# A preactivation convolution on one core: three image rows summed by an overlapping load and VectorE, and output stores issued by GpSimd

## The reference

```python
def _conv(x, w): return lax.conv_general_dilated(x, w, (1, 1), [(1, 1), (1, 1)],
                        dimension_numbers=('NCHW', 'OIHW', 'NCHW'))
# x: (16, 256, 56, 56) f32, conv_w: (256, 256, 3, 3)
v = group_norm(x, G=32, eps=1e-5)
xn = (v - mean(v)) * rsqrt(var(v) + 1e-4) * bn_gamma + bn_beta   # mean, var over n, h, w
t = jnp.where(xn >= 0.0, 1.0, 0.0)
t = jnp.where(xn <= 0.0, -1.0, t)
c_sum = jnp.sum(jnp.clip(xn, -1.0, 1.0) * t, axis=1, keepdims=True)
c_cnt = jnp.sum(jnp.abs(t), axis=1, keepdims=True)
y = _conv(t, conv_w) + conv_b
b_sum = _conv(c_sum, ones(1, 1, 3, 3)) + beta_conv_b
b_cnt = _conv(c_cnt, ones(1, 1, 3, 3)) + beta_conv_b
out = x + y * (b_sum / b_cnt)
```

## Time and profile before

| | before |
|---|---|
| time, median of 3 runs | 962.09 us (962.08 to 962.1) |
| profiled execution, its own time | 963.27 us |
| profiled execution, first to last instruction (span) | 961.4 us |
| busy PE / DVE / ACT / POOL | 798.8 / 784.3 / 587.8 / 106.0 us |
| from 600 to 940 us: PE busy | 340.0 of 340 us |
| HBM read, written | 180.39 MB, 51.78 MB |

### The profile page before, as it was taken

One profiled execution on the slowest core, in us unless ns is written; L12 is line 12 of the kernel. 1 busy time (PEld: TensorE's weight loads), 2 busy tenths in 40 slices (PEclk: granted clock), 3 DMA queues, 4 the chain that ended last, 5 costly groups with the idle time before them and its releaser, 6 DMA issues. The chain is left out here.

```text
span 961.4 us, 13260 instructions
## 1 busy us (share of the span) xinstructions
PE 798.8 (83%) x4750; PEld 469.3 (49%) x4750; DVE 784.3 (82%) x1224; ACT 587.8 (61%) x472; POOL 106.0 (11%) x97
## 2 busy tenths in 40 slices
PE   2100004997999999999999999999999999999996
PEld 2100002554555555555555555555555555555553
DVE  4999997886878787878787878787878787879844
ACT  2043005894777777768686868686868686868410
POOL 0099200000000000000000000000000000000010
PEclk9655556998999999999999999999999999999999
DMA  9999962258979797979798879888888888876697
GB/s 360 431 392 395 412 258 70 71 206 204 298 184 282 189 278 195 273 198 268 207 267 208 261 195 266 219 256 215 254 210 239 233 261 208 264 172 175 158 225 211
DMA packets 41522, 232.41 MB, mean 242 GB/s; under 512 B 8608, under 2 KB 8736, under 8 KB 37408
## 3 DMA queue, kind: packets, MB, share of 16 engines
q1 hardware_dynamic: 31712, 181.43, 51.4%
q0 software_dynamic: 9072, 50.58, 29.0%
q10 hardware_dynamic: 720, 0.18, 0.1%
HBM read 180.39 MB, written 51.78 MB: 241 GB/s over the span
## 5 line engine op out<-in xcount | busy, mean ns | idle before, releaser
L540 PE MATMUL acc<-V,U 128*128 128x385 f16 (+1 forms) x4608 | 776.9, 331 | 17.5 <-DVE V L756 12.1
L540 PEld LDWEIGHTS acc<-V,U 128*128 128x128 f16 x4608 | 449.3, 98 | 333.9 <-issue 16.7
L420 ACT ACTIVATE sn<-acc,inv_s 128x784 f32<-128x784 f32 x128 | 116.7, 913 | 217.0 <-PE acc L540 213.8
L324 POOL DMA_DIRECT2D y<-x x63 | 54.5, 865 | 791.4 <-DVE y L825 774.2
L825 DVE SCALAR_TENSOR_TENSOR y<-y,vec,bmap 128x1568 f32<-128x1568 f32 (+1 forms) x65 | 117.4, 1809 | 8.0 <-DMA bmap<-map_rows 7.8
L399 ACT ACTIVATE r<-xb,ab 128x1568 f32<-128x1568 f32 x64 | 106.5, 1691 | 6.7 <-DVE ssum L763 3.1
L378 ACT ACTIVATE u<-xb,ab 128x1624 f16<-128x1624 f32 x64 | 110.5, 1730 | 0.1
L388 ACT ACTIVATE T<-u 128x1680 f16<-128x1680 f16 x60 | 95.6, 1594 | 5.1 <-DVE D L749 5.0
L390 ACT ACTIVATE T<-T 128x1568 f16<-128x1568 f16 x60 | 90.6, 1511 | 1.9
L749 DVE TENSOR_TENSOR D<-T 128x1568 f16<-128x1568 f16 x64 | 62.4, 975 | 28.5 <-ACT T L390 28.5
L505 PE MATMUL csum<-mv,cst 128*128 128x32 f32 x2 | 0.6, 398 | 94.9 <-DVE mv L625 94.9
(11 more groups left out here) (92 smaller groups left out, 363.6 us busy)
## 6 DMA issues: line engine op xcount, KB each, us to landing
xb<-x SPq DMA_DIRECT2D x64, 812.0 KB, 6.2
y<-x POOLq DMA_DIRECT2D x63, 784.0 KB, 8.2
out<-y SPq DMA_DIRECT2D x63, 784.0 KB, 6.2
y<-x SPq DMA_DIRECT2D x16, 1568.0 KB, 8.3
bmap<-map_rows SPq DMA_DIRECT2D x32, 784.0 KB, 6.0
xb<-x SPq DMA_DIRECT2D x14, 1568.0 KB, 8.6
V<-w_t SPq DMA_DIRECT2D x2, 1152.0 KB, 14.4
out<-y SPq DMA_DIRECT2D x2, 392.0 KB, 2.3
```

The lines of the kernel that those rows point to most:

```text
L420: nc.scalar.activation(sn[:, b, half], acc[:, b, :, 0:N], ACT.Copy, scale=inv_s[:, b:b + 1])\
L540: last = nc.tensor.matmul(by_row(acc[:, g % 2, bank, 0:N])[:, :, lo:hi], U[:, ci, digits, k, dx, co * P:(co + 1) * P], by_row(V[:, a, ci, ...
```

## The change

- `crow` becomes 56 x 3 x 58: one load brings to each partition the row above, its own row and the row below, from overlapping windows of `sum_rows` (`row_windows`). For that `sum_rows` has a row of zeros above and below each image, written once at the start from ScalarE's queue.
- VectorE adds the three rows (`vsum`, a reduction of 3 x 58 values in each partition), then three columns, then bias and count, all in one function `beta_map` where `columns` stood. TensorE's `boxed`, its band matrix and the semaphore `box_done` are gone.
- GpSimd issues the stores of the first 63 pieces: after the accumulating transfer of piece s it waits for that of s - 1 to land and stores piece s - 1. SP's stores of these pieces are gone. SP still stores the two parts of the last one.
- SP's loop over pairs of images is written out.

```diff
-    x_pairs = x_rows[1:NI - 1].rearrange("(i k) c p f -> i k c p f", k=2)
+    row_windows = bass.AP(sum_rows.tensor, 0, [[(H + 2) * W, NI], [W, H], [1, 3 * W]])
...
-        crow = sb("crow", [H, W + 2])
+        crow = sb("crow", [H, 3, W + 2])
+        vsum = sb("vsum", [H, W + 2])
...
-                sp.dma_start(sum_rows[m].rearrange("(h k f) -> k h f", h=2, f=SQ), cs49[:, :, :])\
+                sp.dma_start(sum_rows[m, W:W + H * W].rearrange("(h k f) -> k h f", h=2, f=SQ), cs49[:, :, :])\
                   .then_inc(cs_stored, 16)
                 sp.wait_ge(cs_stored, 16 * m + 16)
-                at_least(sp, hsum_ready, m)
-                sp.dma_start(crow[:, 1:W + 1], sum_rows[m].rearrange("(r w) -> r w", w=W)).then_inc(crow_in, 16)
-
-            def store(n, g):
-                sp.wait_ge(x_added[g], 16 * n + 16)
-                sp.dma_start(out_v[n, g % 2, g // 2], y[:, g]).then_inc(y_out[g], 16)
+                at_least(sp, vsum_ready, m)
+                sp.dma_start(crow[:, :, 1:W + 1], row_windows[m].rearrange("r (k w) -> r k w", w=W))\
+                  .then_inc(crow_in, 16)
...
-                store(n - 1, 0)
                 crow_load(n)
-                store(n - 1, 1)
...
-            with sp.Fori(0, (NI - 4) // 2) as i:
-                image(2 * i + 1, x_pairs[i + 1, 0])
-                image(2 * i + 2, x_pairs[i + 1, 1])
-            image(NI - 3, x_rows[NI - 1])
+            for n in range(1, NI - 2):
+                image(n, x_rows[n + 2])
...
+            def store(s):
+
+                n, g = divmod(s, G4)
+                pool.wait_ge(x_added[g], 16 * n + 16)
+                pool.dma_start(out_v[n, g % 2, g // 2], y[:, g]).then_inc(y_out[g], 16)
+
             for s in range(G4 * NI - 1):
                 n, g = divmod(s, G4)
                 pool.wait_ge(scaled, s + 1)
                 pool.dma_start(y[:, g], x_v[n, g % 2, g // 2], accum_op=ALU.add).then_inc(x_added[g], 16)
+                if s:
+                    store(s - 1)
+            store(G4 * NI - 2)
...
+            act.wait_ge(pads, 4)
+            act.dma_start(sum_rows.rearrange("n (r w) -> n r w", w=W)[:, 0:H + 2:H + 1], crow[0:NI, 0:2, 0:W])\
+               .then_inc(zeros_in, 16)
...
-            def boxed(n):
-
-                pe.wait_ge(hsum_ready, n + 1)
-                at_least(pe, bm_ready, n)
-                nc.tensor.matmul(box[:, 0:W], cst[0:H, C_TRI:C_TRI + P], hsum[:, 1, :],
-                                 start=True, stop=True).then_inc(box_done, 1)
...
-            def columns(n):
+            def beta_map(n):
 
                 dve.wait_ge(crow_in, 16 * n + 16)
-                nc.vector.tensor_tensor(hsum[:, 0, :], crow[:, 0:W], crow[:, 1:W + 1], ALU.add)\
-                  .then_inc(hpart, 1)
+                nc.vector.tensor_reduce(vsum[:, :], crow[:, :, :].rearrange("r k w -> r w k"), AX.X, ALU.add)\
+                  .then_inc(vsum_ready, 1)
+                dve.wait_ge(vsum_ready, n + 1)
+                nc.vector.tensor_tensor(hsum[:, 0, :], vsum[:, 0:W], vsum[:, 1:W + 1], ALU.add).then_inc(hpart, 1)
                 dve.wait_ge(hpart, n + 1)
-                at_least(dve, box_done, n)
-                nc.vector.tensor_tensor(hsum[:, 1, :], hsum[:, 0, :], crow[:, 2:W + 2], ALU.add)\
+                nc.vector.tensor_tensor(hsum[:, 1, :], hsum[:, 0, :], vsum[:, 2:W + 2], ALU.add)\
                   .then_inc(hsum_ready, 1)
-
-            def beta_map(n):
-
-                dve.wait_ge(box_done, n + 1)
+                dve.wait_ge(hsum_ready, n + 1)
                 at_least(dve, bm_stored, 16 * n)
-                nc.vector.scalar_tensor_tensor(
-                    out=bm[:, :], in0=box[0:H, 0:W], scalar=bb[0:H, :], in1=rcount[:, :],
-                    op0=ALU.add, op1=ALU.mult)\
-                  .then_inc(bm_ready, 1)
+                nc.vector.scalar_tensor_tensor(out=bm[:, :], in0=hsum[:, 1, :], scalar=bb[0:H, :], in1=rcount[:, :],
+                                               op0=ALU.add, op1=ALU.mult).then_inc(bm_ready, 1)
```

More of the change, by code:

```diff
@@ L28 @@
 FIRST, SECOND, THIRD = (1, 3), (2, 4), (0, 5)
-C_GROUP, C_TRI, C_COUNT = 0, P, P + P
+C_GROUP, C_COUNT = 0, P
 C_FOLD = C_COUNT + W
@@ L111, in conv_preact @@
         y_out = [sem(f"y_out{g}") for g in range(G4)]
+        last_out = [sem(f"last_out{k}") for k in range(2)]
         x_added = [sem(f"x_added{g}") for g in range(G4)]
@@ L126, in conv_preact @@
                              "cs_stored", "crow_in"))
-        hpart, hsum_ready, box_done, bm_ready, bm_stored = (
-            sem(s) for s in ("hpart", "hsum_ready", "box_done", "bm_ready", "bm_stored"))
+        zeros_in = sem("zeros_in")
+        vsum_ready, hpart, hsum_ready, bm_ready, bm_stored = (
+            sem(s) for s in ("vsum_ready", "hpart", "hsum_ready", "bm_ready", "bm_stored"))
         bmap_in = [sem(f"bmap_in{h}") for h in range(2)]
@@ L231, in map_load @@
                 sp.dma_start(bmap[:, h, :],
-                             map_rows[bass.ds(n, 1), h * HPX:(h + 1) * HPX].to_broadcast([P, HPX]))\
+                             map_rows[n:n + 1, h * HPX:(h + 1) * HPX].to_broadcast([P, HPX]))\
                   .then_inc(bmap_in[h], 16)
@@ L251, in image @@
                     load(n, ahead, 1)
-                store(n - 1, 2)
                 map_load(n, 1)
@@ L255, in image @@
                     load(n, ahead, 2)
-                store(n - 1, 3)
                 if ahead is not None:
@@ L261, in _ @@
                 first_load(g)
+            sp.wait_ge(zeros_in, 16)
             crow_load(0)
@@ L267, in _ @@
                 load(0, x_rows[2], g)
-            with sp.Fori(0, (NI - 4) // 2) as i:
-                image(2 * i + 1, x_pairs[i + 1, 0])
-                image(2 * i + 2, x_pairs[i + 1, 1])
-            image(NI - 3, x_rows[NI - 1])
+            for n in range(1, NI - 2):
+                image(n, x_rows[n + 2])
             image(NI - 2)
             image(NI - 1)
-            for g in range(3):
-                store(NI - 1, g)
             for k, (lo, hi) in enumerate(LAST_PARTS):
                 sp.wait_ge(last_added, k + 1)
-                sp.dma_start(out_v[NI - 1, 1, 1][:, 4 * lo:4 * hi], y[:, 3, 4 * lo:4 * hi]).then_inc(y_out[3], 16)
+                sp.dma_start(out_v[NI - 1, 1, 1][:, 4 * lo:4 * hi], y[:, 3, 4 * lo:4 * hi]).then_inc(last_out[k], 16)
             for g in range(G4):
-                sp.wait_ge(y_out[g], 16 * (NI + (g == 3)))
+                sp.wait_ge(y_out[g], 16 * (NI - (g == 3)))
+            for k in range(2):
+                sp.wait_ge(last_out[k], 16)
         @block.gpsimd
@@ L589, in _ @@
             third(0, 0, 1)
-            boxed(0)
             second(0, 0, 2)
@@ L615, in _ @@
             nc.vector.memset(u[:, :, 0:UR:UR - 1], 0.5).then_inc(pads, 1)
-            nc.vector.memset(crow[:, :], 0.0).then_inc(pads, 1)
+            nc.vector.memset(crow[:, :, :], 0.0).then_inc(pads, 1)
             nc.vector.memset(eps[:, 0:1], GN_EPS)
@@ L658, in _ @@
             nc.vector.tensor_scalar(mxb[:, :], mxb[:, :], 2.0 ** -14, None, ALU.mult).then_inc(wrow, 1)
-            nc.vector.memset(crow[:, 0:1], 0.0).then_inc(wscale, 1)
+            nc.vector.memset(hsum[:, 0, 0:1], 0.0).then_inc(wscale, 1)
             for k in range(8, 12):
@@ L848, in _ @@
             transform(1, 1, 0)
-            columns(0)
+            beta_map(0)
             ends(0, 1)
-            beta_map(0)
             pair_sum(1, 0)
@@ L882, in image @@
                     if g == 0:
-                        columns(n)
+                        beta_map(n)
                     if prep and g == 1:
@@ L915 @@
     rows = np.arange(H)
-    consts[:H, C_TRI:C_TRI + H] = abs(rows[:, None] - rows[None, :]) <= 1
     near = 3.0 - (rows == 0) - (rows == H - 1)
@@ L931 @@
     args = {name: nc.dram_tensor(name, v.shape, F32, kind="ExternalInput").ap() for name, v in arrays.items()}
-    sum_rows = nc.dram_tensor("sum_rows", (NI, H * W), F32, kind="Internal").ap()
+    sum_rows = nc.dram_tensor("sum_rows", (NI, (H + 2) * W), F32, kind="Internal").ap()
     map_rows = nc.dram_tensor("map_rows", (NI, H * W), F32, kind="Internal").ap()
```

4 lines of the change are left out of this document (removed).

## The result

| | before | after |
|---|---|---|
| median of the runs | 962.09 us (961.41 to 962.1, 4 runs) | 949.62 us (949.5 to 950.02, 4 runs) |
| ratio to before | | 0.987, 95% interval 0.9858 to 0.9881 |
| profiled execution, its own time | 963.27 us | 950.02 us |
| span | 961.4 us | 948.0 us |

The change takes 12.5 us, where 13.1 were forecast, and the time is 949.62 us, where 949.0 were.

What follows compares the result with a forecast made beforehand. TensorE, busy 48.70 of 48.70 us an image, was taken as the bound. Savings 6.4 + 7.2 - 0.5 = 13.1 us took the profiled 963.27 to 950.2; with the runs' median 1.2 lower, 949.0, range 947.0 to 956.5.

Steps and rivals of the forecast that it cites:

- TensorE's product: Line 526 leaves TensorE's stream: 0.46 us in each of images 2 to 15, 6.4 us saved.
- Image 1: TensorE's stall before the third group (4.40 us) and the half clock behind it (2.78 us) go: 7.2 us saved.
- The rows' lateness: The load of three pieces a partition reaches VectorE 0 to 3.5 us later, taken as 1; cost 0.
- rival D: Rows load 5.7 us later than before, so TensorE waits in slot 1 of every image: 969 us; chance 0.06.
- VectorE's slack of 4.4 us: In slot 1 the rows may be used 4.4 us later before TensorE loses anything: 2.44 + 2.3 - 0.33.
- The reduction: VectorE's new sum over three rows, 174 values in 56 partitions, takes 0.33 us.
- GpSimd's stores: Issue of 0.86 us hidden, waits for additions hold up nothing, 2.2 us of DMA engines a store: cost 0.
- rival C: Stores in q0 take 4.3 us each, some 12 images become bound by transfers: 958 us; chance 0.06.
- my list of signs that the forecast is wrong: TensorE waiting in the steady part, period over 48.3 us, VectorE waiting for `y_out`, or GpSimd's last store landing after piece 63's parts.
- The end: Last pieces' stores, with slower issue by GpSimd, cost 0 to 2.7 us, taken as 0.5.
- A: Image 1 keeps its stall and half clock: 956.2 us; chance 0.12.
- B: VectorE and ScalarE do not follow the faster TensorE, each image's 0.46 us returns as a wait: 955.4 us; chance 0.06.

Runs made afterwards that it cites:

- e6_extra_fp32_product: The changed kernel plus one fp32 product of 56x56 on resident constants, result unread, in slot 1 of images 1 to 15: 957.06 us.
- e3_sp_stores_sums_first: The changed kernel with output stores back on SyncE in the old order, except that image 1's sums go ahead of the first output store: 949.86 us.
- e1_sp_stores: The changed kernel with the output stores back on SyncE in the old order, the three-row sum staying on VectorE: 956.41 us.
- e9_store_before_next_add: The changed kernel with GpSimd waiting for each piece's addition and storing that piece ahead of the next addition: 954.83 us.
- e4_rows_loaded_twice: The changed kernel with SyncE loading each image's three rows twice, only the second load releasing VectorE: 950.44 us.
- e5_rows_loaded_three_times: The changed kernel with SyncE loading each image's three rows three times in turn, only the last load releasing VectorE: 967.64 us.

## Why the prediction was right, point by point

**TensorE's product, 6.4 us: right.** The 0.46 us came from two stretches of the timeline, and the period fell by 0.46 us (48.706 to 48.246); from image 2 to the last group TensorE takes 6.46 us less. An extra product on resident data costs 0.46 us in the period, 0.48 by the medians (e6_extra_fp32_product).

**Image 1, 7.2 us: right, with its mechanism.** From the first group of image 1 to the sums' products of image 2 TensorE takes 7.18 us less. The sums left at 213.85, where 213.8 was forecast. That it was the place in SyncE's order is shown by e3_sp_stores_sums_first. One sentence of this step was too easy: that TensorE needs only `ends` in time and would not need the rows. That is true only as long as VectorE does not wait long for them. e1_sp_stores leaves the wait of 7.18 us in place, and 4.53 us of it reach TensorE.

**The rows' lateness: inside its range, mis-sized and put down to the wrong transfer.** I put the rows 1 us later (0 to 3.5), for a load of three pieces; it is 2.4. The load takes no longer: from its issue to VectorE's use of the rows there are 1.6 us in the loop before (568.81 to 570.37) and 1.7 after (559.65 to 561.33). The sums' store takes 2.3 us more, for a reason that I had listed only under rival D: GpSimd's store lies among its packets. e9_store_before_next_add shows it. Together the rows are used 2.4 us later than before, 8.7 us after the sums' products and not 6.3 (561.33 - 552.64 against 617.35 - 611.07).

**VectorE's slack of 4.4 us: right.** 2.4 us are used by the change and 2.1 are left. e4_rows_loaded_twice stays below, e5_rows_loaded_three_times, at nearly rival D's numbers, measures 967.64 us where D had 969.

**The reduction: right**, 0.33 to 0.35 us against 0.33.

**GpSimd's stores: no cost, as forecast, though two sizes were off.** A store takes 7.3 / 4 = 1.8 us of the DMA engines in q0, below the 2.2 of q1 and far from rival C's 4.3. The additions land later than I had them, in 9.2 us (14.6 at most) and not 8.2 (11.4). The stores land in 9.3 us (14.5 at most) and not 6.0. These are an addition and the store behind it, one image in the middle:

```profile
550.24 0.84 POOL L325 DMA_DIRECT2D y<-x  x1 [12.24 <-DVE y L818]
550.78 0.87 POOL L320 DMA_DIRECT2D out<-y  x1
```

The store's row begins 0.54 us after the addition's, so both are issued in 1.4 us and not in 1.7. VectorE waits for a store (`y_out`, line 795) twice, 3.4 us in all, 3.1 of them in image 15. That was on my list of signs that the forecast is wrong; TensorE does not notice. GpSimd does wait for landed additions, seven times, 28.8 us in all, where I had said that this wait holds up nothing; the time shows no cost of it.

**The end: mis-sized by 0.5 us.** I took 0.5 and it is nothing: 949.11 to 961.4 before, 935.69 to 948.0 after. The last store goes out ahead of the first part, and from that part's issue to the end of the span there are 4.8 us in both. These are the last store of GpSimd and SyncE's parts of the last piece:

```profile
941.14 0.55 POOL L320 DMA_DIRECT2D out<-y  x1 [5.59 <-DMA y<-x]
...
943.21 2.29 SPq L272 DMA_DIRECT2D out<-y  x2
```

The last store's issue takes 0.55 us and starts 2.1 us ahead of the first part's. The Trainium skill's rule (SBUF — State Buffer, section "A bandwidth-pool intuition that's wrong"), by which it would have come 2.2 us later (an estimate from the page's 3100 ns), does not show: GpSimd issues it at 941.14, in the same moment as VectorE's line 818, in 0.55 us. VectorE's instruction there is not the copy that the page measured.

**Rivals.** None of the four happened: clock 1.00, and no wait of TensorE from 223.20 us to its last group (A, B, D); a store takes 1.8 us of the DMA engines and not 4.3 (C).

**The number: in part luck.** The forecast for the runs was 0.6 us low. The profiled executions differ by 13.25 us, the medians by 12.5; that 0.7 us lies between executions and is not resolved by these runs. With the end at nothing the sum is 13.6 us and the forecast 948.5, 1.1 us low: the wrong 0.5 us of the end brought it closer.

## What to carry to other kernels

Where an engine runs without a gap, price an instruction from two stretches of its timeline that hold it a different number of times, and everything else by whether its slack is larger than its delay: here 4.2 us of waiting on VectorE were free and 6.0 us cost a whole kernel its gain. An engine that issues transfers in order and waits between them holds up what stands behind. Here the place in that order was worth 6.5 us (956.41 against 949.86) and the choice of the queue nothing, so look at what stands ahead of the first small transfer that somebody waits for, in the first turns of a loop above all, before moving work to another queue. And when the bound is one engine's stream, look for its smallest instructions that come in pairs.

## What the runs showed of the hardware

Two fp32 products of 49 weight columns cost TensorE 0.41 us between fp16 products, one of 98 columns 0.12 us, the 56x56 one 0.46 us. What makes the last one dearer than the wide one is open; it was not tried.

A 12 KB store to HBM in q1 is waited for 3.3 us in the kernel before, where one addition is under way in q0, 5.8 us in the kernel after, where an output store stands behind the addition there, and 3.5 us where that store went out earlier (e9_store_before_next_add from 500 us on) or was not in q0 (e3_sp_stores_sums_first). These are means; in the kernel before the longest is 5.1 us.

Waits of TensorE of some microseconds did not always bring the lower clock, and it did not always last as long. After 3.62 us of waiting in the kernel before the granted clock was 0.50 from 230.76 until 237 us; after 4.53 us in e1_sp_stores it was back at 1.00 by 244, 4.4 us after the wait ended. In e5_rows_loaded_three_times the 132 products behind a wait of 3.18 us took 22.09 us, the full clock.

The issue of a GpSimd store takes 0.56 us when it waited for its semaphore and 0.86 us right behind an addition (median 863 ns of 63); but there it begins 0.54 us after the addition's, while that row is still open.
